# Graph-layers kernel: head flips by DMA in fp16 halves, f32 queries and keys, normalising on ScalarE

## What is computed

```
q, k, v = heads(h @ Wq + bq), heads(h @ Wk + bk), heads(h @ Wv + bv)      # layer 0
scores = q @ k.T / sqrt(32) + beta * adj;  scores = where(adj > 0, scores, -9e15)
x = x + softmax(scores) @ v

q, k, v = heads(x @ Wq.T), heads(x @ Wk.T), heads(x @ Wv.T + bv)          # layer 5
a = q @ k.T * 384 ** -0.5 + adj;  rows of a that are all zero give zeros
out = h + softmax(a) @ v @ Wo.T + bo
```

## Time and profile before

| | |
|---|---|
| median of 3 runs | 2871.72 us (2871.25 to 2871.86) |
| the profiled execution | 2870.44 us, its span 2868.4 us |
| PE busy | 2745.3 us |
| VectorE (DVE) busy | 2475.5 us |
| ScalarE (ACT) busy | 1797.9 us |
| GpSimd (POOL) busy | 1396.4 us |
| granted TensorE clock, mean | 0.991 of full speed |

### The profile page before, as it was taken

One profiled execution on the slowest core, in us unless ns is written; L12 is line 12 of the kernel. 1 busy time (PEld: TensorE's weight loads), 2 busy tenths in 40 slices (PEclk: granted clock), 3 DMA queues, 4 the chain that ended last, 5 costly groups with the idle time before them and its releaser, 6 DMA issues.

```text
span 2868.4 us, 86681 instructions
## 1 busy us (share of the span) xinstructions
PE 2745.3 (96%) x33152; PEld 2100.0 (73%) x33152; DVE 2475.5 (86%) x6886; ACT 1797.9 (63%) x6516; POOL 1396.4 (49%) x2313
## 2 busy tenths in 40 slices
PE   3799999999999999999999999999999999999996
PEld 2577777777777777777777777777777777777763
DVE  6788888888888888888888888888888888888875
ACT  6566666666666666666666666666666666666653
POOL 0345554554544554554554554554455454554553
PEclk8999999999999999999999999999999999999998
DMA  6221121221212121121221222121121221121110
GB/s 199 57 38 40 39 42 40 38 42 41 37 43 42 36 45 39 36 45 39 36 45 39 36 45 40 39 42 40 39 42 40 39 42 39 36 45 40 36 32 20
DMA packets 343428, 125.40 MB, mean 44 GB/s; under 512 B 310896, under 2 KB 342896, under 8 KB 342896
## 3 DMA queue, kind: packets, MB, share of 16 engines
q1 hardware_dynamic: 333808, 107.28, 18.9%
q10 hardware_dynamic: 9216, 12.59, 1.2%
HBM read 31.72 MB, written 12.58 MB: 15 GB/s over the span
## 4 chain that ended last, share of the span: by engine, by line
PE 85%; DVE 6%; ACT 3%; issue 2%; POOL 2%; DMA 2%; SPq 0%; POOLq 0%; ACTq 0%; DVEq 0%
PE bank L925 63%; PE bank L1030 8%; PE bank L975 5%; PE bank L991 3%; PE bank L967 3%; DMA ht<-qk 1%; PE bank L1021 1%; ACT t L672 1%; DVE t L804 1%; PE bank L980 1%; PE bank L997 1%; DVE qk L782 1%; DMA row<-in_rows_dram 1%; DVE qk L750 1%; ACT qk L648 0%
## 5 line engine op out<-in xcount | busy, mean ns | idle before, releaser
L925 PE MATMUL bank<-w_hi,ht 128*128 128x384 f16 x3840 | 1028.6, 326 | 0.2 <-ACT v L639 0.2
L925 PE MATMUL bank<-ht,w_hi 128*128 128x128 f16 x9216 | 838.4, 220 | 17.1 <-DMA ht<-qk 15.3
L925 PE MATMUL bank<-ht,w_lo 128*128 128x128 f16 x4608 | 806.5, 220 | 0.0
L925 PEld LDWEIGHTS bank<-ht,w_hi 128*128 128x128 f16 x9216 | 725.9, 98 | 79.1 <-issue 33.8
L925 PE MATMUL bank<-w_lo,ht 128*128 128x384 f16 x1920 | 626.5, 326 | 0.0
L672 ACT ACTIVATE t<-t,few 128x128 f32<-128x128 f32 x1536 | 592.4, 389 | 6.8 <-DVE few L813 4.9
L925 PEld LDWEIGHTS bank<-w_hi,ht 128*128 128x128 f16 x3840 | 375.8, 98 | 232.8 <-issue 2.0
L925 PEld LDWEIGHTS bank<-ht,w_lo 128*128 128x128 f16 x4608 | 453.5, 98 | 0.0
L551 POOL TENSOR_TENSOR h<-h,row 128x384 f32<-128x384 f32 x256 | 258.0, 1008 | 242.8 <-DVE h L904 242.8
L663 ACT ACTIVATE qk<-bank 128x256 f16<-128x256 f32 x576 | 215.6, 381 | 234.9 <-PE bank L925 234.3
L541 POOL TENSOR_TENSOR v<-v,row 128x384 f32<-128x384 f32 x256 | 259.4, 1014 | 180.9 <-ACT v L639 180.9
(11 more groups left out here) (112 smaller groups left out, 5059.7 us busy)
## 6 DMA issues: line engine op xcount, KB each, us to landing
x<-in_x_dram SPq DMA_DIRECT2D x64, 192.0 KB, 2.3
out_dram<-h ACTq DMA_DIRECT2D x64, 192.0 KB, 2.2
ht<-qk SPq DMA_TRANSPOSE x384, 2.8
w_hi<-in_weights_dram SPq DMA_DIRECT2D x9, 576.0 KB, 5.1
w_lo<-in_weights_dram SPq DMA_DIRECT2D x8, 576.0 KB, 4.9
adj<-in_adj_dram SPq DMA_DIRECT2D x64, 64.0 KB, 2.2
row<-in_rows_dram SPq DMA_DIRECT2D x1, 3456.0 KB, 15.4
spare<-in_weights_dram SPq DMA_DIRECT2D x2, 576.0 KB, 5.0
```

What stands on the lines that cost most here:

```text
L925: m = nc.tensor.matmul(out, a, b, start=(first and n == 0), stop=(last and n == 3 * len(left) - 1))
```

## The change

- **Flips by DMA.** `flip` and `flop` are now SP's. After `exp` a new step `split` makes two fp16 halves of four heads: ScalarE writes the high half (PH, in the place of qk), VectorE the low half (PL, in the place of t). SP's `flip` transposes the high half by DMA from qk into t (PTH), `flop` the low half from t into qk (PTL); a flop waits until the flip of the same four heads has landed, as it overwrites that flip's source. Each is one transfer of 128x512 fp16, three and three per attention.
- **Mix in halves.** PE's `mix` is 36 fp16 matmuls instead of 12 f32 ones, and waits for all flops. The values are kept as halves (VH): for GAT out of the bank, their bias being added by GpSimd to x; for GRAPHORMER by a new step `vsplit` out of h.
- **Queries and keys in f32.** ScalarE writes them once (QF), VectorE's part of `proj` is gone, and the scores are 12 f32 matmuls instead of 36 fp16 ones.
- **Normalising.** VectorE computes only -mean * rstd (128x1); ScalarE normalises.
- `vals` comes ahead of `scores`, and all fixed orders are written anew.

```diff
+WHOLE_QK = (GAT, GRAPHORMER,)
...
@@ -60,21 +61,22 @@
                 add("proj", layer, m)
         if layer in ATTENTION:
             for g in range(G):
+                add("vals", layer, g)
+            if layer == GRAPHORMER:
+                add("vsplit", layer, 0)
+            for g in range(G):
                 add("scores", layer, g)
-            for g in range(G):
-                add("vals", layer, g)
-            end = "back" if layer == GAT else "project"
-            for g in range(G):
-                for c in range(C):
-                    add("exp", layer, (g, c))
-                for c in range(C):
-                    add("flip", layer, (g, c))
-                if layer == GRAPHORMER:
-                    add("scale", layer, g)
-                if g > 0:
-                    add(end, layer, g - 1)
-                add("mix", layer, g)
-            add(end, layer, G - 1)
+            for c in range(C):
+                add("exp", layer, (0, c))
+                if c > 0:
+                    add("split", layer, (0, c - 1))
+            add("split", layer, (0, C - 1))
+            for name, c in (("flip", 0), ("flip", 1), ("flop", 0), ("flip", 2), ("flop", 1), ("flop", 2)):
+                add(name, layer, (0, c))
+            if layer == GRAPHORMER:
+                add("scale", layer, 0)
+            add("mix", layer, 0)
+            add("back" if layer == GAT else "project", layer, 0)
         elif layer in (DIR_A, DIR_B):
...
 BODY = {
     "tensor":
-        "041143333231203032011221214404144303434033320202102204444342314143122332320010200414040144431313"
...
+        "011333332424303022202004414434313441333222122444443030414133313110020040424002444333233000004141"
...
-        return ["normed"]
+        return ["shift", "centred"]
...
+        if name == "proj":
+            return layer not in WHOLE_QK
+        return name not in ("flip", "flop", "finish", "aturn") and not (name == "context" and directed)
...
-        return name in ("load", "turn", "proj", "vals", "exp", "scale", "flip", "mix", "gram", "aturn", "context",
+        return name in ("load", "norm", "turn", "proj", "vals", "vsplit", "exp", "split", "scale", "mix", "gram", "aturn", "context",
...
+    return name in ("load", "turn", "flip", "flop")
...
-        PT = [t[:, 0] for t in T]
         flat_qk = [q[:].rearrange("p w c a t -> p (w c a t)") for q in QK]
         PARTS = [q.bitcast(F32).rearrange("p (h k) -> p h k", h=H) for q in flat_qk]
-        RT = [q[:, 2 * D:4 * D].bitcast(F32).rearrange("p (c k) -> p c k", c=C) for q in flat_qk]
-
-        few = [sb(f"few{s}", [P, G * (6 + 2 + 7 + 4 * H)]) for s in range(STREAMS)]
+        RT = [h[:, 0].rearrange("p (c k) -> p c k", c=C) for h in HN]
+        VH = [v[:, 0].bitcast(F16).rearrange("p (a d) -> p a d", a=2) for v in V]
+        QF = [q.bitcast(F32).rearrange("p (c a t) -> p c a t", c=C, a=2) for q in flat_qk]
+        PH = [q.rearrange("p (c x) -> p c x", c=C) for q in flat_qk]
+        halves = [t[:, 0].rearrange("p h k -> p (h k)").bitcast(F16).rearrange("p (c a x) -> p c a x", c=C, a=2) for t in T]
+        PL = [t[:, :, 0] for t in halves]
+        PTH = [t[:, :, 1].rearrange("p c (h k) -> p c h k", h=HPC) for t in halves]
+        PTL = [q.rearrange("p (c h k) -> p c h k", c=C, h=HPC) for q in flat_qk]
...
+        flip_in = [[sem(f"flip_in{s}_{odd}") for odd in range(2)] for s in range(STREAMS)]
+        flop_in = [sem(f"flop_in{s}") for s in range(STREAMS)]
...
+        def wait_flipped(eng, r, s, layer, c):
+
+            layers = 2 * r + ATTENTION.index(layer)
+            eng.wait_ge(flip_in[s][c % 2], 16 * ((layers + 1) if c == 1 else (2 * layers + c // 2 + 1)))
...
+                elif name == "flip":
+                    wait_for(sp, r, s, "high", ("split", layer, i))
+                    wait_for(sp, r, s, "low", ("split", layer, i))
+                    sp.dma_start_transpose(PTH[s][:, i[1]], PH[s][:, i[1]]).then_inc(flip_in[s][i[1] % 2], 16)
+                elif name == "flop":
+                    wait_flipped(sp, r, s, layer, i[1])
+                    sp.dma_start_transpose(PTL[s][:, i[1]], PL[s][:, i[1]]).then_inc(flop_in[s], 16)
...
+                elif name == "vals" and layer == GAT:
+                    wait_for(pool, r, s, "centred", ("norm", layer, i))
+                    wait_row(pool, r, ROW_V[layer][0])
+                    nc.gpsimd.tensor_tensor(X[s][:, 0], X[s][:, 0], row[:, ROW_V[layer][0], :],
+                                            ALU.add).then_inc(done[s]["biased"], 1)
...
+                    wait_for(pool, r, s, "low", ("vsplit", layer, 0))
...
+                elif name == "vals" and layer == GAT:
+                    wait_filled(act, r, s, step)
+                    nc.scalar.activation(VH[s][:, 0], bank_of(r, s, step)[:, 0:D], ACT.Copy,
+                                         scale=1.0 / WS).then_inc(done[s]["high"], 1)
...
+                elif name == "vsplit":
+                    wait_for(act, r, s, "biased", ("vals", layer, i))
+                    nc.scalar.activation(VH[s][:, 0], HN[s][:, 0], ACT.Copy).then_inc(done[s]["high"], 1)
...
+                elif name == "norm":
+
+                    wait_for(act, r, s, "shift", step)
+                    if layer == GAT and i == 0 and r > 0:
+                        act.wait_ge(stored[s], 16 * r)
+                    nc.scalar.activation(HN[s][:, i], X[s][:, i], ACT.Identity, bias=NM[s][:, i:i + 1],
+                                         scale=RS[s][:, i:i + 1]).then_inc(done[s]["centred"], 1)
...
+                        dst = QF[s] if layer in WHOLE_QK else QK[s][:, 0]
                         for side in range(2):
-                            last = nc.scalar.activation(QK[s][:, 0, i, side], bank_of(r, s, step)[:, side * TOK:(side + 1) * TOK],
+                            last = nc.scalar.activation(dst[:, i, side], bank_of(r, s, step)[:, side * TOK:(side + 1) * TOK],
...
+                elif name == "split":
+
+                    g, c = i
+                    wait_for(act, r, s, "exped", ("exp", layer, i))
+                    if layer == GRAPHORMER:
+                        wait_for(act, r, s, "sums", ("scores", layer, g), C + 1)
+                    nc.scalar.activation(PH[s][:, c], T[s][:, 0, HPC * c:HPC * (c + 1)].rearrange("p h k -> p (h k)"),
+                                         ACT.Copy).then_inc(done[s]["high"], 1)
...
-                elif name == "flip":
-
-                    g, c = i
-                    wait_filled(act, r, s, step)
-                    nc.scalar.activation(PT[s][:, HPC * c:HPC * (c + 1)].rearrange("p h k -> p (h k)"),
-                                         bank_of(r, s, step)[:, :], ACT.Copy).then_inc(done[s]["evicted"], 1)
...
-                    nc.vector.tensor_scalar(HN[s][:, i], X[s][:, i], MV[s][:, i, 0:1], RS[s][:, i:i + 1], ALU.subtract,
-                                            ALU.mult).then_inc(done[s]["normed"], 1)
+                    nc.vector.scalar_tensor_tensor(out=NM[s][:, i:i + 1], in0=MV[s][:, i, 0:1], scalar=-1.0, in1=RS[s][:, i:i + 1],
+                                                   op0=ALU.mult, op1=ALU.mult).then_inc(done[s]["shift"], 1)
...
+                elif name == "split":
+
+                    g, c = i
+                    wait_for(v, r, s, "high", step)
+                    low_half(PL[s][:, c], T[s][:, 0, HPC * c:HPC * (c + 1)].rearrange("p h k -> p (h k)"),
+                             PH[s][:, c]).then_inc(done[s]["low"], 1)
+                elif name == "vsplit":
+                    wait_for(v, r, s, "high", step)
+                    low_half(VH[s][:, 1], HN[s][:, 0], VH[s][:, 0]).then_inc(done[s]["low"], 1)
...
+                elif name == "vals" and layer == GAT:
+                    wait_filled(v, r, s, step)
+                    wait_for(v, r, s, "high", step)
+                    nc.vector.scalar_tensor_tensor(out=VH[s][:, 1], in0=bank_of(r, s, step)[:, 0:D], scalar=1.0 / WS,
+                                                   in1=VH[s][:, 0], op0=ALU.mult, op1=ALU.subtract).then_inc(done[s]["low"], 1)
...
-                    wait_for(pe, r, s, "low", ("proj", layer, C - 1))
+                    wait_for(pe, r, s, "high" if layer in WHOLE_QK else "low", ("proj", layer, C - 1))
                     cols = slice(i * P, (i + 1) * P)
                     for c in range(C):
+                        if layer in WHOLE_QK:
+                            for h in range(HPC):
+                                rows_h = slice(HD * h, HD * (h + 1))
+                                m = nc.tensor.matmul(bank_of(r, s, step, h)[:, c * P:(c + 1) * P], QF[s][rows_h, c, 0, cols],
+                                                     QF[s][rows_h, c, 1, cols], start=True, stop=True)
+                                if c == C - 1:
+                                    m.then_inc(filled[s], 1)
+                            continue
...
-                elif name == "flip":
```

(19 more changed lines are left out.)

## The result

The changed kernel takes 3200.5 us, the median of four runs (3182.9 to 3209.5), against 2871.8 before (2871.3 to 2872.4). The ratio is 1.114, with a 95% interval from 1.109 to 1.119. It is slower by 329 us, and the time lies outside the predicted range of 2700 to 2860.

What follows compares the result with a forecast made beforehand. It took PE to be full, with a floor of 2713 us after 157 less PE work. With VectorE near full too, 410 us per 10 graphs gave 2870.4 - 108 + 5 = 2767, rounded to 2765 us; range 2700 to 2860.

Steps and rivals of the forecast that it cites:

- PE's two steps: On PE, 128 steps each: the fp16 mix saves 20 us, the f32 scores cost 32 us more.
- rival 2: PE's scores: f32 loads in row strips go one after another, 2.64 us a step, 2955 us; chance 0.10, mild form 0.05.
- 2713: PE's floor in us: 2870.4 less 157, if PE stayed as full as before.
- the term of the flips: On PE: 1536 transposes leave, at 0.110 us each, 169 us less.
- the bound of 120: VectorE's work: upper bound of its forecast change, +65 us (+15 to +120).
- the one on SP and the DMAs: SP's queue and transfers: 768 transposes more, neither a bound; longer path hidden except +5 us at the end.
- The size: SP's issue time for a 128x512 transpose: 0.81 to 1.21 us, taken as 0.85.
- The test: SP at 18 of 41 us per graph and queue 1 under 40%: neither is a bound.
- The cover: Path from last exp to mix: about 5 us longer per attention, hidden by the order in the steady state.
- The gain assumed without SP: PE and VectorE in steady running: 410 us per 10 graphs, 108 us less over some 60 graphs.
- Rival 1: VectorE and PE fill each other's time badly: 422 us per 10 graphs, 2834, taken as 2800 to 2860; chance 0.17.
- Rival 3: SP: two of a graph's six turns come 2.8 us late and PE idles; half showing, 2944 us; chance 0.05.

Runs made afterwards that it cites:

- e1: The changed kernel without its 768 flips and flops, the mix reading unflipped halves: 2927.6 us, ratio 1.020.
- e2: The changed kernel with each flip and flop as one plain DMA of the same bytes, nothing transposed: 2931.4 us, ratio 1.021.
- e9: The changed kernel with one flip and one flop of 128x1536 per attention instead of three each: 3104.9 us, ratio 1.082.
- e12: The changed kernel without flips and flops, VectorE making only 32 of each 512 columns of the heads' low halves: 2870.5 us, ratio 1.000.
- e10: The changed kernel flipping the high halves only, the low halves read unflipped: 2951.1 us, ratio 1.028.
- e6: The changed kernel with three plain DMAs in place of each flip and flop, same bytes together: 3672.0 us, ratio 1.279.

## Why the prediction was wrong

**PE's two steps were right, its sum wasn't.** Before, a mix took 0.59 us from first to last start and 0.205 to the next work (medians of 128); now 0.467 and 0.152: 0.18 less, 0.16 predicted. The scores went from 0.469 and 0.147 to 0.680 and 0.203: 0.27 more, 0.25 predicted. The row strips run together with f32 too, so rival 2 is out. But PE's busy time came to 2715.9 us, and to 2651.5 in e1, where "near 2600" was forecast. (2713 was a time, with PE's idle time of before in it, and isn't what 2715.9 is to be held against.) In e1 with the clock at 1.00, in a stretch as long as 10 graphs take there:
```profile
317.00:752.00 435.00, 407.14 (x4912) 298.59 (x4912) 391.01 (x1056) 307.26 (x1055) 225.55 (x356) 1.00 0.19 40
```
PE is busy for 407 us there (409 in a later one), where the sum had 399, down from 424. So PE's work fell by some 16 us per 10 graphs, or 100 over the kernel, and not by 157. As the mix and the scores are as forecast, what is left is the term of the flips, 169 us; no run measures it alone, and a record lasts until its result arrives, so that each pause of PE adds a little to its busy time. PE is idle for 484 us from its first instruction on, 99 before.

**VectorE's** low halves cost 706 ns, 690 predicted. Its sum is +111 us instead of +65, inside the bound of 120. The edge product is most of the rest, 59.6 us instead of the 23.2 it took before (932 ns for 362). The traces show why: 53 of its 64 instructions now run while GpSimd does its 128x384 addition to h (L589), and take 1.05 us each; the 11 others take 0.35. Before, one did, and took 1.06 us; the 63 others took 0.35. Per 10 graphs VectorE is busy for 397 us, 388.5 forecast. **ScalarE** came to 2024 instead of 1964: a normalising costs it 704 ns, not 520, so +47 us. It had room.

**The step that failed is the one on SP and the DMAs.** It had three parts.
- *The size*: "a shorter one costs 0.81 to 1.21, I take 0.85". Measured 1.21 and 1.27, at the upper bound and past it. Nothing had spoken for a price that falls with the columns; 1536 columns cost 1.43. SP had 23 us of issuing per graph, not 18.
- *The test*: "Neither is a bound", from 18 us in 41. An average share says that a queue isn't full. It doesn't say that what waits in it isn't late. Flips and flops come six at a time, and the turns of four other streams stand among them in a fixed order. Nor does the share sort the runs: at 37% e2 lost 4 us, and at 33% e9 lost 177.
- *The cover*: "In the steady state the order hides this", so the longer path was put at nothing but 5 us at the end. From the last low half to the mix the prediction counted two landings, 4.6 to 5.6 us. It is 9.0 us, as SP's issuing and waiting in its queue stand in it too, and the order has room for 6.0 (GAT) and 8.3 (GRAPHORMER). For turns the cover is thin: before, PE takes ht 4.3 to 7.7 us after SP starts on it (medians of the six turns), of which 2.8 are its landing. In the changed kernel it takes it after 2.9 to 5.2. In e1 it is 2.9 to 4.8, so it is the new orders that took this slack, and not the flips; the flips put delays on top, which PE then pays.

**The gain assumed without SP was wrong too.** "I take 410 us per 10 graphs": with no flips at all, e1 needs 435 (two passes of 217.4), had 428. There PE is busy for 408 us and VectorE for 392 (means of two stretches), so PE has 27 us of pauses where 11 were assumed, and 9 us more of work. Rival 1's 422 was the nearest. e12 shows that taking 154 us of work from VectorE gives back 57.

**The rivals.** Rival 3, slower by SP, came true, with a chance of 0.05. Its mechanism, late turns with PE waiting for ht, is there: that wait grew by 94 us from e1 to the changed kernel. The late flops, with 130 us of waiting, are the larger part, and the rival doesn't have them. Its size was 179 us on top of 2765; the flips cost 273 on top of 2928. What spoke against it were two rows that can't bear on it: DMA's 2% of the chain, and SP's 2057 us of waiting. Both tell of a queue with 8 us of work per graph. They say nothing of one with 23.

**The clock** followed PE's idle time. Its mean fell from 0.991 to 0.965, as PE idled more: PE stood at half its clock for 224 us of the span, 51 before. In e2 and e10 the mean is back at 0.985 and 0.986. In e6, with PE idle the most, it is 0.901, which may be part of why the cost grows faster than SP's load; no run parts the two.

No kernel of this study is faster than the one before; e12, which leaves work out, equals it. Of the three parts, f32 queries and keys cost 11 us and the normalising 79, each alone in the old orders, against the kernel before as measured beside it. Moving the flips to SP didn't pay here even with the flips left out, in these orders.

## What to carry to other kernels

Cost a DMA by three numbers, the time on the queue that issues it, the landing, and the transfer, and take the first from a row of the same kind: here it hardly depends on the size, so few large transfers are cheap for the queue, but they put whole landings in a row into the path. Before putting work on a queue that others depend on, add up the whole path through it, issues and places in the queue included, and hold it against the slack that its reader has in the fixed order; the busy share answers neither. And when all orders are fixed, work taken from a full engine isn't time gained until something shows that the others keep up.

## What wasn't expected of the hardware

- The transposing DMA holds SP for 1.19 us at least for 512 columns, 1.21 for 768 and 1.28 for 1536 (medians 1.21 to 1.29 and 1.43), while a plain DMA of 128x512 takes 0.46 at least and 0.47 (flips) or 0.60 (flops) in the median. The landing does grow: 2.5 us for 512 columns, 2.8 for 768, 3.7 to 4.0 for 1536.
- Single issues took up to 2.95 us, in the kernel before up to 2.46 (2.27 in the stretch of the earlier trace rows).
- ScalarE needs 704 ns to normalise 128x384 with scale and bias per partition in f32, where VectorE took 482 and a plain ScalarE copy to fp16 of the same size 519.
- A VectorE instruction of 128x128 f32 that takes 0.35 us alone took 1.05 us beside GpSimd's 128x384 addition, in 53 of 64 cases of the changed kernel.
